# Loading the halves of experts 4 to 7 on GpSimd's DMA queue in place of SyncE's

## The reference

```python
x = x + xattn(layernorm(x), ctx_2048, Wq, Wg, bg, Wkv, Wo)
# xattn: q, k, v projections, kv_summary = sum over s of k v^T per head,
#        out = (q kv_summary / (q ksum + eps)) * sigmoid(x Wg^T + bg) @ Wo^T
x = x + ffn(layernorm(x), Wr, We, be)
# ffn:
logits = jnp.einsum('bsd,de->bse', x, Wr)
w, sel = jax.lax.top_k(logits, 2)
w = jax.nn.softmax(w, axis=-1)
for e in range(8):
    out = out + gate[..., e:e + 1] * (jnp.einsum('bsd,df->bsf', x, We[e]) + be[e])
```

## Time and profile before

| | |
|---|---|
| median of 3 runs | 614.5 us (614.04 to 616.86) |
| the profiled execution | 615.09 us, of which the span in the profile is 613.5 us |
| PE busy | 560.7 us, 91% of the span |
| DVE, ACT, POOL busy | 323.3, 198.6, 166.4 us |
| PE's share of the chain that ended last | 65%, the DMAs' 11% |
| PE's clock, mean over the span | 0.975 of full speed |

### The profile page before, as it was taken

How to read it: one execution, slowest core, us unless ns; L and a number is a source line. 1 busy time by engine, 2 the same in 40 slices (tenths; PEclk the granted TensorE clock), 3 DMA queues, 4 the chain that set the end, 5 groups by cost and what they waited for, 6 DMA issues and landing times.

```text
span 613.5 us, 10482 instructions
## 1 busy us (share of the span) xinstructions
PE 560.7 (91%) x2944; PEld 469.5 (77%) x2945; DVE 323.3 (53%) x889; ACT 198.6 (32%) x348; POOL 166.4 (27%) x193
## 2 busy tenths in 40 slices
PE   6999997999999999999999999995999999998750
PEld 4888886788887878887887888884878788776540
DVE  4553275356337736533763642773466544457653
ACT  5455332433533353444243344422211111111100
POOL 3014654303632131356030152001022000056313
PEclk9999999999999999999999999998799999999995
DMA  8713345602452061253234125869967558789956
GB/s 281 285 35 109 132 147 197 240 35 105 168 175 103 9 230 68 103 203 105 103 94 163 51 103 204 303 197 403 413 196 238 171 169 277 240 242 363 386 191 188
DMA packets 44427, 113.87 MB, mean 186 GB/s; under 512 B 4976, under 2 KB 4976, under 8 KB 43504
## 3 DMA queue, kind: packets, MB, share of 16 engines
q1 hardware_dynamic: 24240, 57.43, 27.7%
q0 software_dynamic: 11232, 39.85, 18.2%
q10 hardware_dynamic: 8928, 16.26, 6.9%
HBM read 66.86 MB, written 46.66 MB: 185 GB/s over the span
## 4 chain that ended last, share of the span: by engine, by line
PE 65%; DMA 11%; issue 4%; POOL 3%; DVE 2%; ACT 1%; POOLq 0%; SPq 0%; DVEq 0%; ACTq 0%
PE pj L1097 17%; PE pj L1099 17%; PE pj L1098 17%; DMA khat<-xs 5%; PE kvb L1151 4%; PE tp L1089 4%; PE tp L1159 3%; PE pj L1105 2%; PE pj L1179 2%; POOL aux L531 1%; DMA out_dram<-wraw 1%; DMA wraw<-in_L_ffn_We_dram 1%; DMA we_halves<-aux 1%; DMA qhat<-y,gidx 1%; DMA num<-y,gidx 1%
## 5 line engine op out<-in xcount | busy, mean ns | idle before, releaser
L1097 PE MATMUL pj<-R 128*128 128x512 f32 x448 | 184.7, 412 | 9.8 <-DVE R L804 9.8
L1099 PE MATMUL pj<-R 128*128 128x512 f32 x448 | 177.0, 395 | 0.0
L1098 PE MATMUL pj<-R 128*128 128x512 f32 x448 | 175.9, 393 | 0.0
L1097 PEld LDWEIGHTS pj<-R 128*128 128x128 f32 x448 | 85.0, 190 | 26.7 <-DVE R L804 11.6
L1099 PEld LDWEIGHTS pj<-R 128*128 128x128 f32 x448 | 84.7, 189 | 19.1
L1098 PEld LDWEIGHTS pj<-R 128*128 128x128 f32 x448 | 85.3, 190 | 15.4
L1097 PE MATMUL pj<-R,aux 128*128 x184 | 77.1, 419 | 5.1 <-DVE zeros L1013 2.5
L1099 PE MATMUL pj<-R,aux 128*128 x184 | 73.0, 397 | 0.0
L1098 PE MATMUL pj<-R,aux 128*128 x184 | 72.6, 395 | 0.0
L714 ACT CAST aux<-tp 128x512 fp32r<-128x512 f32 x46 | 26.9, 586 | 118.7 <-PE tp L1159 118.7
L869 DVE SCALAR_TENSOR_TENSOR khat<-buf,khat 128x512 f32<-128x512 f32 x32 | 25.7, 803 | 69.7 <-ACT buf L673 69.7
(11 more groups left out here) (160 smaller groups left out, 740.4 us busy)
## 6 DMA issues: line engine op xcount, KB each, us to landing
we_halves<-aux POOLq DMA_DIRECT2D x14, 1024.0 KB, 5.1
R<-we_halves SPq DMA_DIRECT2D x7, 2048.0 KB, 11.1
khat<-xs SPq DMA_DIRECT2D x46, 256.0 KB, 3.2
wraw<-in_L_ffn_We_dram POOLq DMA_DIRECT2D x16, 512.0 KB, 6.5
buf<-in_ctx_dram SPq DMA_DIRECT2D x15, 512.0 KB, 3.5
y<-kvbd ACTq DMA_DIRECT2D x23, 256.0 KB, 3.6
y<-zeros ACTq DMA_DIRECT2D x23, 256.0 KB, 3.4
wraw<-in_x_dram SPq DMA_DIRECT2D x4, 1024.0 KB, 7.7
```

The source lines that it names most:

```text
L1097: nc.tensor.matmul(bank[:, :], s_hi(k), m_hi(k), start=(k == 0), stop=False)
L1098: nc.tensor.matmul(bank[:, :], s_hi(k), m_lo(k), start=False, stop=False)
L1099: last = nc.tensor.matmul(bank[:, :], s_lo(k), m_hi(k), start=False, stop=(k == KT - 1))
```

## The change

The four `load_halves` calls of experts 4 to 7 leave SP's program. They are issued by POOL, between and behind its four `scale` steps of the last batch: expert 4 after `scale` 0 and the wait for the last gate projection, expert 5 after `scale` 1, experts 6 and 7 after `scale` 3 and the wait for the last output projection. That second wait stood ahead of the memset before and is only moved. What is loaded, from where and to where stays as it was.

```diff
--- before.py
+++ after.py
@@ -391,15 +391,10 @@
             sp.wait_ge(SEMS["qhat"], nth("qhat", B - 1, G - 1))
             for e in range(E):
                 sp.dma_start(be_all[:, e, :], be[e:e + 1, :].broadcast_to((P, D))).then_inc(be_loaded, 16)
-            sp.wait_ge(SEMS["g"], nth("g", B - 1, TT - 1))
-            load_halves(4)
-            load_halves(5)
             load_tile(0, 2, 0)
             sp.wait_ge(SEMS["wo"], nth("wo", B - 1, TT - 1))
             load_tile(0, 3, 1)
-            load_halves(6)
             load_tile(0, 4, 0)
-            load_halves(7)
             sp.wait_ge(x2_stored, 16 * B)
             sp.wait_ge(SEMS["x2"], nth("x2", B - 1, TT - 1))
             load_x2r(4, 4, x2r_loaded[1])
@@ -573,13 +568,24 @@
                 pool.wait_ge(wx_loaded[e - 1], 16)
                 pool.sem_inc(we_ready, 2)
 
+            def load_halves(e):
+
+                pool.dma_start(R[:, 2 * e:2 * e + 2, :, :].rearrange("p a k d -> p (a k d)").bitcast(F32), wx_dram[e, :, :]).then_inc(wx_loaded[e - 1], 16)
+
             halves_in(1)
-            for t in range(TT):
-                scale(1, t, 1, "_x2", last, t)
+            scale(1, 0, 1, "_x2", last, 0)
+            pool.wait_ge(SEMS["g"], nth("g", last, TT - 1))
+            load_halves(4)
+            scale(1, 1, 1, "_x2", last, 1)
+            load_halves(5)
+            scale(1, 2, 1, "_x2", last, 2)
+            scale(1, 3, 1, "_x2", last, 3)
+            pool.wait_ge(SEMS["wo"], nth("wo", last, TT - 1))
+            load_halves(6)
+            load_halves(7)
             halves_in(2)
             halves_in(3)
             halves_in(4)
-            pool.wait_ge(SEMS["wo"], nth("wo", last, TT - 1))
             nc.gpsimd.memset(bias[:, :], 0.0).then_inc(zeroed, 1)
             halves_in(5)
             halves_in(6)
```

## The result

The changed kernel takes 623.24 us as the median of 4 runs (621.79 to 623.86), beside 615.68 us (614.04 to 618.17, 4 runs) for the kernel before. The ratio is 1.0114, with a 95% interval of 1.0083 to 1.0146: it is slower, by 7.6 us by the medians and by 7.0 us by the ratio. The profiled execution took 623.73 us, of which the span is 622.2.

What follows compares the result with a forecast made beforehand. The prediction took PE's 8.1 us wait for tile 2, a bandwidth wait in queue order, plus 3.1 us of lowered clock, as the bound. 615.1 us profiled + 8 = 623.1, 0.6 above the median, so 622.5; range 606.5 to 625.

Steps and rivals of the forecast that it cites:

- What bounds the kernel: PE's 8.1 us wait for tile 2 behind queued loads, plus 3.1 us of slow clock; no wait at all would give -11.2.
- SP's and POOL's issues cost nothing: Tile 2 still issued near 415.2 on SP, gain nothing; POOL's four issues, 0.71 us each, fit around the `scale` steps.
- A turn is one packet, and POOL's packets are 16 KB: On the shared DMA engines q0 gets 8 bytes for each byte of q1, whose `be` and tile packets are 2 KB.
- The first rival: POOL's packets are 4 KB and nothing changes: +0.6 us, or up to -3; best 614 us; chance 0.20.
- All four halves are served before tile 2: Four experts' halves pass ahead of tile 2 where two did: +8 us, between +5.9 and +9.7.
- The count on the way there: Near 423 us, `be` and tile 2 still have about 41 of 72 packets per DMA engine; halves 6 and 7 need 16 turns.
- The clock is paid as before: PE's clock falls in tile 2's wait as before, costing the same 3.1 us up to tile 3's turn.
- DVE's wait for `be`: Ends near tile 2's landing; the low half of tile 1 fits in tile 2's turn: 0, at most +0.7 us.
- The sum: 615.1 us of the profiled execution + 8 = 623.1; that execution stood 0.6 above its median, so 622.5.
- the likeliest case: Tile 2 lands behind all four halves: 620 to 625 us, forecast 622.5; chance 0.57.
- What would show it: Tile 2 lands in 22 to 24 us, PE's wait about 16, `be` median over 15, no further tile wait of PE.
- The second rival: Tile 2 gets through and the kernel is faster: -7.3 us, or -11.2 with no wait; best 605 us; chance 0.23.

Runs made afterwards that it cites:

- experiment 8: Kernel before, halves spread behind the tiles on SP's queue: 608.42 us in 1 MB pieces, 610.03 in whole 2 MB, 616.26 (beside 621.41) in 512 KB quarters.
- experiment 3: Changed kernel with the four halves issued on ScalarE's hardware queue in place of POOL's: 622.21 us, ratio 1.0085 to the kernel before.
- experiment 1: Changed kernel with each of POOL's halves cut into four DMAs of 4 KB runs: 616.99 us, ratio 1.0022 to the kernel before.
- experiment 5: Changed kernel with POOL issuing halves 6 and 7 only once tile 2 has landed: 620.48 us, ratio 1.0054 to the kernel before.
- experiment 4: Changed kernel with tile 2 loaded on ScalarE's queue, where nothing stands ahead of it: 622.17 us, ratio 1.0097 to the kernel before.
- experiment 7: Kernel before with tile 2's load issued ahead of halves 4 and 5 on SP's queue: 617.88 us, ratio 1.0030.

## Why the prediction was right

- *What bounds the kernel.* Tile 2's wait, with the clock behind it: taking the wait away wins 7.4 us (experiment 8, 1 MB pieces), of the 11.2 that it was priced at. The rest is given back in new waits.
- *SP's and POOL's issues cost nothing.* Right. Tile 2 is issued right behind tile 0's turn as before, and each `scale` still starts only when DVE's variances are there.
- *A turn is one packet, and POOL's packets are 16 KB.* Right, and the second half was open: 266 packets against 265, 3.83 MB against 0.48. The 16 KB were a choice between two values that no row decided, at 0.57 against 0.20 for the 4 KB case. (Where the prediction says of the page's 4096 B that by it "the second rival below" holds, it means the first in its list, that of 4 KB packets.) As for even turns, they held for POOL's queue at all three sizes, but not for ACT's queue with 16 KB packets (experiment 3). The first rival had the right arithmetic for the other size: with 4 KB it said +0.6 us in the wait, and experiment 1 has 9.47 - 8.08 = +1.4, and a ratio of 1.0022.
- *All four halves are served before tile 2.* Right. It was priced at +8 between bounds of +5.9 and +9.7; the wait grew by 8.56 us. The +8 was picked between the bounds, so that it came this near is in part luck. Experiment 5 takes this term away: with two halves held back, tile 2's wait is 6.85 us.
- *The count on the way there* came out near by two errors that offset each other. At 423 us q1 had 1.22 MB of `be` and tile 2 left, 37 packets for each DMA engine; the prediction said 41. But it had `be` served from 410 on, while most of the loads of tiles 0 and 1, 16 packets for each engine, still stood ahead of it: tile 1, issued at 410.1, took 8.3 us to land, in the kernel before 3.0. And halves 5, issued at 416.10, moved nothing before about 420.5, 4.4 us later, where the prediction had 1.7. From 417 to 420.7 q1 was nearly alone on the engines and moved 0.96 MB, where the prediction gave all such gaps together 15 packets for each engine, 0.49 MB. Why halves 5 started so late no run shows. The view of 418.5 to 422.5 us has most of the gap:

```profile
q1 hardware_dynamic: 530, 0.96, 66.9%
q0 software_dynamic: 37, 0.61, 35.3%
```

- *The clock is paid as before.* Right within 0.5 us: 7.11 us in place of 7.57 from tile 2's turn to tile 3's.
- *DVE's wait for `be`.* It ended at 439.85, just ahead of tile 2's turn at 440.47, and cost nothing of its own. Experiment 4 shows that it stands directly behind: take tile 2 out of the backlog and PE waits for `be` in its place.
- *The sum.* 622.5 us forecast, 623.24 measured. The difference to the kernel before, forecast as 8.0, is 7.6 by the medians and 7.0 by the ratio. The forecast stood on a median of 614.5 for the kernel before; with a fourth run that is 615.68, so part of the agreement within 0.7 us is chance. The range, 606.5 to 625, took in nearly every case that was considered; it is the likeliest case and its mechanism that were borne out.
- *What would show it.* PE took tile 2 23.5 us after its issue (22 to 24 expected to land). The view of 412 to 416 us has 90 packets and 1.47 MB on q0 against 74 and 0.15 MB on q1, as expected. The median landing of `be` rose from 5.0 to 13.5 us, less than the 15 expected. And PE did wait on tiles after tile 2, four times, 1.8 us in all, all of them after 450 us; the kernel before has 2.4 us of such waits there.
- *The second rival* (the faster one) said that a 256 KB load on a queue of its own passes 16 KB packets in 5.5 us. In experiment 4 such a load took 11.7 us. It also took for possible that a wait of 3.9 us leaves the clock up; in experiment 5 a wait of 3.29 us did not. So its 7.3 us would probably have come out smaller.

By the Trainium skill, "DMA: Bandwidth & Descriptors", section "SWDGE vs HWDGE vs iDMA", a packet from GpSimd has preferably at most 4096 B. In this case that held for runs of 2 and 4 KB (the earlier trace rows and experiment 1); runs of 8 and 16 KB went as packets of their own size, as the profile counts packets.

The Trainium skill, on the same page, section "Queues, rings and completion order", has each DMA engine deal its turns between queues by packet. The 266 and 265 agree with that; the 194 and 299 of experiment 3 do not fit even turns.

## What to carry to other kernels

In these runs, moving a large load to another queue did not put it behind the small loads of the first: POOL's and SP's queues took turns by packet, and long contiguous runs won against short rows by the ratio of their sizes (eight bytes to one at 16 KB against 2 KB). On ACT's queue the ratio was less, 5.4 to one, and the loss no smaller that could be told. Look in the DMA view for a stretch in which both queues are full and compare packets and bytes; if something that an engine waits for stands in a backlog of small packets, cut the runs of the other load, start it later, or spread it in pieces behind the small loads on the same queue. Here runs of 4 KB took the loss away where 8 KB did not, the later start took away the added wait but not all of the loss, and only the spreading beat the kernel before. Price such a move by the bytes that are ahead of the load that is waited for, and ask of every reordering which later load then has those bytes ahead.

## What the runs showed of the hardware

- Packets beside 2 KB packets of q1, both queues full: POOL's queue with 16 KB 266 to 265, with 8 KB 455 to 457, with 4 KB 445 to 442. ACT's hardware queue with 16 KB: 194 to 299, not equal.
- POOL's queue moved nothing for halves 5 until about 4.4 us after their issue in the changed kernel.
- PE's clock fell in a wait of 3.29 us (experiment 5), while the long wait of the kernel before had lasted about 4.1 us when it fell. Here is the stretch with the wait, and the one after it:

```profile
446.50:450.81 4.31, 1.02 (x8) 0.86 0.99 353
450.81:457.57 6.76, 6.76 (x25) 0.59 0.49 162
```

- A mean of 0.86 over 4.31 us is 1.2 us at half speed, so it fell some 2.1 us into this wait. In the two waits of experiment 7, 5.74 us at a mean of 0.70 and 4.80 us at 0.87, it fell 2.3 and 3.6 us in. With whole 2 MB (experiment 8) it fell 1.8 us after the end of a wait of 1.80 us, with another 0.34 us idle in between, and a wait of 1.85 us earlier in the same run left it up. The time that a wait may last at full clock isn't fixed by these runs. After a wait of 16.6 us the slow stretch was no longer than after one of 8.1 us.
